# A new order of turns on four engines for a kernel of eight transformer stages

## What is computed

```python
for l in range(4):
    sa, ca, ga, sb, cb, gb = modulation(silu(c[l]) @ wmod[l])     # per batch element
    x = x + ga * attn[l](layernorm(x) * (1 + ca) + sa)
    x = x + gb * ffn[l](layernorm(x) * (1 + cb) + sb)
# attn: 0 decayed linear attention (a scan over tokens, gamma)
#       1 four blocks of causal linear attention with 16 heads of 8, each with a 512-wide MLP
#       2 delta rule with a fixed decay, 3 gated delta rule (both solve a triangular system per chunk)
# ffn:  0 and 1 mixture of 8 experts, 2 of them per token, 2 and 3 one expert per batch element
```

## Time and profile before

| | |
|---|---|
| Median of three runs | 1737.48 us (1735.43 to 1738.29) |
| Span of the profiled execution | 1734.0 us |
| Instructions in the profile | 31,744 |
| PE busy | 1698.0 us, 98% |
| DVE busy | 1234.6 us, 71% |
| POOL busy | 1218.5 us, 70% |
| ACT busy | 1088.9 us, 63% |
| HBM traffic | 22.52 MB read, 2.15 MB written |

### The profile page before, as it was taken

The page is one execution under the profiler, slowest core; times in us unless marked ns, Lnnn a source line. Parts: engine busy times, 40 slices in busy tenths (PEclk is TensorE's granted clock), DMA queues, the critical chain, the costliest instruction groups (busy, mean ns, idle before and its releaser), DMA issues.

```text
span 1734.0 us, 31744 instructions
## 1 busy us (share of the span) xinstructions
PE 1698.0 (98%) x10006; PEld 1300.6 (75%) x10006; DVE 1234.6 (71%) x4490; ACT 1088.9 (63%) x2904; POOL 1218.5 (70%) x1771
## 2 busy tenths in 40 slices
PE   8999999999999999999999999999999899999998
PEld 5788888876667676676666677767788787788976
DVE  7864335688987988988899866445566766578773
ACT  6555226556677678777776786446546666665656
POOL 5655649898878987888789785135347876666667
PEclk9999999999999999999999999999999999999999
DMA  7100000010000000000000000000000001000002
GB/s 254 71 29 1 1 2 3 3 51 1 1 1 1 1 1 1 1 1 1 1 1 1 1 11 6 1 1 7 2 3 3 1 18 31 21 1 2 2 2 73
DMA packets 24027, 26.70 MB, mean 15 GB/s; under 512 B 3492, under 2 KB 20772, under 8 KB 23476
## 3 DMA queue, kind: packets, MB, share of 16 engines
q1 hardware_dynamic: 23860, 24.67, 4.4%
HBM read 22.52 MB, written 2.15 MB: 14 GB/s over the span
## 4 chain that ended last, share of the span: by engine, by line
PE 80%; POOL 6%; DVE 6%; ACT 4%; issue 2%; DMA 0%; SPq 0%; POOLq 0%; ACTq 0%; DVEq 0%
PE ps L87 74%; PE ps L90 7%; POOL arena L104 6%; ACT arena L98 4%; DVE arena L104 2%; DVE arena L110 1%; DVE arena L130 1%; DVE arena L147 1%; ACT arena L99 0%; DVE arena L133 0%; ACT L98 0%; DVE arena L107 0%; DMA arena<-in_x 0%; DVE arena L136 0%; DVE ps L147 0%
## 5 line engine op out<-in xcount | busy, mean ns | idle before, releaser
L104 POOL TENSOR_TENSOR arena<-arena 128x512 f32<-128x512 f32 (+6 forms) x836 | 715.5, 869 | 278.4 <-DVE arena L110 96.9
L98 ACT ACTIVATE arena<-ps 128x128 f32<-128x128 f32 (+11 forms) x1204 | 338.6, 326 | 394.1 <-PE ps L87 287.8
L87 PE MATMUL ps<-arena 128*128 128x128 f32 (+4 forms) x2792 | 441.0, 291 | 10.0 <-DVE arena L104 3.5
L87 PEld LDWEIGHTS ps<-arena 128*128 128x128 f32 x2792 | 373.3, 191 | 97.9 <-issue 46.5
L104 DVE TENSOR_TENSOR arena<-ps,arena 128x128 f32<-128x128 f32 (+4 forms) x696 | 312.9, 468 | 176.0 <-PE ps L87 163.6
L98 ACT ACTIVATE arena<-arena 128x128 f32<-128x128 f32 (+1 forms) x836 | 321.2, 439 | 51.3 <-POOL arena L104 39.6
L87 PE MATMUL ps<-arena,moe 128*128 128x256 f32 (+1 forms) x960 | 288.2, 439 | 0.0
L87 PE MATMUL ps<-arena,cst 128*128 128x504 f32 (+2 forms) x768 | 283.6, 489 | 2.2 <-ACT arena L98 1.1
L98 ACT ACTIVATE arena<-ps,cols 128x512 f32<-128x512 f32 x324 | 216.8, 688 | 103.3 <-PE ps L87 96.5
L104 POOL TENSOR_TENSOR arena<-arena,cst 128x144 f32<-128x144 f32 (+7 forms) x536 | 186.2, 356 | 93.0 <-ACT arena L98 57.4
L110 DVE SCALAR_TENSOR_TENSOR arena<-ps,arena 128x128 f32<-128x128 f32 (+1 forms) x476 | 156.6, 364 | 120.4 <-PE ps L87 94.2
(11 more groups left out here) (120 smaller groups left out, 1756.5 us busy)
## 6 DMA issues: line engine op xcount, KB each, us to landing
rows<-in_rows SPq DMA_DIRECT2D x1, 2253.0 KB, 14.2
arena<-in_x SPq DMA_DIRECT2D x8, 256.0 KB, 5.3
wf<-in_wf SPq DMA_DIRECT2D x2, 1024.0 KB, 6.6
arena<-in_L_ffn_W SPq DMA_DIRECT2D x8, 256.0 KB, 2.9
out_dram<-arena SPq DMA_DIRECT2D x8, 256.0 KB, 2.7
wmod<-in_wmod SPq DMA_DIRECT2D x4, 384.0 KB, 7.7
arena<-kept SPq DMA_DIRECT2D x24, 64.0 KB, 2.9
arena<-kept SPq DMA_DIRECT2D x8, 192.0 KB, 3.0
```

What stands on the lines that cost most here:

```text
L87: return UNSENT if self.e is None else self.e.matmul(out, lhsT, rhs, start=start, stop=stop)
L98: return self.e.activation(out, in_, func, bias=bias, scale=scale)
L104: return UNSENT if self.e is None else self.e.tensor_tensor(out, a, c, op)
```

## The change

The four strings of `TURNS` are replaced, and nothing else. They were found by annealing on durations from a trace, with the SBUF port that VectorE and GpSimd share counted as exclusive, so that two instructions that need it don't run at once. The strings for `pe`, `dve`, `act` and `pool` go from 3333, 3861, 2145 and 1180 digits to 3303, 3831, 2115 and 1150. What falls away are digits whose generator had already ended: every element's work is still emitted in full.

```diff
-    "pe": ("2000000000000120002230001222000112200011100211012003013211003031110332001332322330320113213131222121"
+    "pe": ("0000210000000020003220001222000121010101022010112003011310020111330330201323213203331231130212232111"
```

More of the change, by code:

```diff
@@ new lines @@
+    "act": ("4002440103400202122021211101120333033341123210000033040010100000120032212003302010110020222203202103"
+          "3020112103231213011213223101301122112011113201221021113321211113120223112332301003032103000113000120"
+          "3003120013001030212301300232230010301000202110221032203030011103122333310100200222001212101011200200"
+          "2220203313011231123221202030030302111312333112302302002333031111320311212022231313131110213322022103"
+          "1233323003000013013331113032021222003212200301333311320103301033301033122221212002203020322133011131"
+          "2133023313020223313102121111032301222113230031211000020222311213133231031230021002022003121311130233"
+          "2312223112111000100302323323131012211011102030331302230300222230211131130323113020220011210223033313"
+          "2213030110000013123222230323300310111032210221020130002011100011110203022332101101100210022220211123"
+          "3110302130300020033213222013231111332302223020302302102211311123320210002101322111121303210323330301"
+          "2022122232131111320330200312222022110113231313130232122210302330330310101301113331330322221323102333"
+          "3023011132102032100003023303321222112310002000133120200002201202323031102302000320221231301322022112"
+          "1231113332233032122112111001000121221123221111200300201233332223212203113331112131101032202221002001"
+          "2203003300313010301201023101130023110231011302131021013001103012231033301232202000102322103233010310"
+          "3212300220113010132002332310033333322311231123111221303012223221133121011313103022223320322203210023"
+          "0322022310320202311301311003232331001122330003200332312313202013333300303123200303303333120331220001"
+          "1202113022110112212222011331023022310110323101300032123200313003322131112011300002303330002232233230"
+          "1210103113330201011233121322013320210102231211111203022021131323321223130003121313300123220033112033"
+          "1112333223210131203333100302213331100232231103033221020210320122003313230113120111302330313030333120"
+          "0121020220032001313223310121103313103213132113122011330221332233221313022031220300330222032131022303"
+          "3300210032132101210121003110012313202222110220021123011033030123221303302023113202113221133111233112"
+          "2031233322203110322322333233310331202031233320000012011110113320100132221001122121033223133321323332"
+          "230300222312333"),
```

190 lines of the change are left out of this document (84 added, 106 removed).

## The result

The changed kernel takes **1778.28 us** in the median of four runs (1775.58 to 1778.51), the kernel before 1736.45 in the runs beside it. The ratio is 1.0236, with an interval of 1.0222 to 1.0251, so the change costs 42 us. The forecast was 1729.8, and its range ended at 1744. Both the sign and the size were wrong.

A forecast was written before the change was run, and what follows sets the result against it. PE was taken as the bound, busy for 1698.0 of 1734.0 us. The terms summed to -7.7 us, giving a span of 1726.3 us and, with 3.5 us for the median, 1729.8 us; the range was 1716 to 1744.

The forecast's parts named there:

- New waits: On PE, the reshuffle creates five new waits of 0.45 us among some 2670 waiting places: +2.0 us.
- A: Rival: no change, 1737.0 us; waits move rather than vanish, delays reaching PE through DVE and POOL; chance 0.23.
- Waits with more cover: 31 of PE's 62 waits get more work of other elements ahead of them; half of 18.8 us won: -9.4 us.
- The two named places: PE's waits at the `wo` matmul near 1110 us and the l2 matmul near 1366 us, 0.46 us each, would go.
- Waits with less cover: 9 of PE's 62 waits get less work of other elements ahead of them: +4.0 us.
- Short stalls: Fewer waiting instructions right behind one of their own element, 733 to 629 on PE: -3.0 us.
- The start: ACT's table load moves into its idle time before 14.62 us; PE gains up to 1.0, pays up to 0.4: -0.4 us.
- The shared port: DVE and POOL instructions lengthening each other on SBUF, an estimated 16 us in both engines, would count little: -1.0 us.
- Table loads: Two more table loads of 1.28 us on ACT, which holds 4% of the chain: +0.1 us.
- B: Rival: slower, 1746 us; keeping all port pairs apart delays nearly full POOL from 1340 to 1410 us; chance 0.17.
- C: Rival: much faster, 1715 us; the order takes two thirds of 32.8 us of PE's waits, 22 us; chance 0.10.

The follow-up runs named there:

- r: The old strings with some 175 swaps of neighbouring steps drawn at random and unpriced, 3% of the steps: 1777.79 us.
- h3: The old order for the first 150 us, the changed kernel's order behind it: 1777.4 us.
- g: Strings annealed from the old order with the shared port counted as exclusive for certain DVE and POOL instructions, delays counted in full: 1748.45 us.
- p1: Strings annealed from the old order with PE's round trip alone counted too short: 1799.19 us.
- c: Strings annealed from the old order with the port counted but the round trips of all engines priced short: 1831.11 us.
- a: Strings annealed from the old order on a replay fitted to the traces, with all delays and the shared port counted: 1741.45 us.
- b: Strings annealed from the old order with all delays counted but the shared port left out: 1746.17 us.
- d: Strings annealed from the changed kernel's order instead of the old one, with all delays and the port counted: 1738.26 us.
- e: Strings annealed from the old order with 0.04 us more counted on each handing over between engines: 1742.58 us.
- p2: Strings annealed from the old order with results of DVE, ACT and POOL counted ready too early, PE's round trip in full: 1761.09 us.
- h1: The new order for what the old one starts in its first 867 us, the old order behind it: 1752.93 us.
- h2: The old order for the first 867 us, the new order behind it: 1762.81 us.

## Why the prediction was wrong

**New waits** (+2.0 us, bounds 0 and 18.8) is the step that failed. I took five, and there are 92 newly idle instructions with 44.0 us. With the lateness too short to show as idle, what wasn't a wait before grew by 57.9 us. Even the upper bound was wrong, since it took the waits removed as the measure of those that can be made. The measure should have been the places where one can arise, the "2670 waiting places" of the same paragraph, where r shows how much there is to lose: an unpriced swap of neighbours costs 41.6 / 175 = 0.24 us on average. The new waits arose mostly at producers that found their engine busy with other elements' work (199 of the 271 newly late instructions, 45.6 of 58.4 us). The prediction looked at what stands on PE, and put nothing down for the reshuffled strings of DVE, ACT and POOL, although its rival A names that path.

**Waits with more cover** (-9.4) held, and was even small. By the count of PE instructions since the element's last, 41 of the 93 idle ones have more ahead of them, and their lateness went from 21.4 to 6.3 us, -15.1. The two named places are among them. The `wo` matmul starts without a wait:

```profile
1132.78 0.72 PE L87 MATMUL ps<-moe,arena 128*128 128x128 f32 x5
1133.34 0.39 PE L87 MATMUL ps<-wo,arena 128*128 128x128 f32 x2
```

The l2 matmul of the earlier trace rows does too, inside a run of eighteen:

```profile
1393.04 2.21 PE L87 MATMUL ps<-arena 128*128 128x128 f32 x18
```

But the matmul of element 0 just ahead of it, which had 0.10 us of idle time before it at 1366.36, now waits 0.35 us.

**Waits with less cover** (+4.0) had the wrong sign: 16 instructions, from 5.9 to 5.4 us. What has already waited isn't what a reshuffle makes wait.

**Short stalls** (-3.0) rested on the fall of adjacent waiting places from 733 to 629, and that measure misleads. PE's late instructions rose from 189 to 310 while it fell. It takes an element's cover on PE as whole instructions, of 0.11 us or so each, and ignores what runs on the engine that must supply the next one. Of the 92 newly idle instructions, 49 have less cover than before, but 25 have the same and 18 have more. The example at 1286 us is one of the 18. Among the other engines POOL idles 131.6 us ahead of the layer norms' L104, 128.4 of it for DVE's L147 (93.0 and 89.2 before), and ACT's L98 from SBUF 70.9 instead of 51.3. These rows alone prove little: POOL's idle time grew by 43.8 us in all, about as much as the span, and ahead of its largest group it fell from 278.4 to 252.0.

```profile
L98 ACT ACTIVATE arena<-arena 128x128 f32<-128x128 f32 (+2 forms) x836 | 320.2, 439 | 70.9 <-POOL arena L104 63.5
...
L104 POOL TENSOR_TENSOR arena<-arena,mhalf 128x4 f32<-128x4 f32 (+1 forms) x140 | 150.2, 1073 | 131.6 <-DVE arena L147 128.4
```

**The start** (-0.4) was read right on ACT and wrong on PE. The table load ran where I put it and the second read ended at 15.57 us, before 17.0:

```profile
12.91 1.28 ACT L98 ACT_TABLE_LOAD   x1
14.21 0.20 ACT L98 ACTIVATE gd<-rows 128x1 f32<-128x1 f32 x1
14.32 1.25 ACT L98 ACTIVATE arena<-ps,cols 128x512 f32<-128x512 f32 x2
```

Before, the same stretch of PE was this:

```profile
12.45 3.75 PE L87 MATMUL ps<-arena,w 128*128 128x512 f32 x4 [0.87 <-ACT arena L98]
16.03 0.61 PE L90 MATMUL ps<-cst,arena 128*128 128x128 f32 x4
17.45 0.49 PE L87 MATMUL ps<-w,arena 128*128 128x128 f32 x2 [0.81 <-ACT arena L98]
```

The wait at 17.45 for ACT's second read is gone, and that matmul starts at 15.62. The transposes, at 16.03 before and 15.04 now, gained 1.0 us too, but not by the load. Before, they followed without a wait on the four matmuls of 12.45, which took 3.75 us at a granted clock of 0.50 (from 10 to 14 us; 0.74 from 14 to 18). Those take 1.98 us now, at 1.00, and then PE waits 1.26 us for the first read, which stands behind the load. That the gain came out as large as forecast is luck. Then PE waits longer, 2.00 us at 18.43, and after that its clock is down, which the prediction had excluded from 20 us on. Here are PE's timeline and the windows at the start of the changed kernel:

```profile
11.80 1.98 PE L87 MATMUL ps<-arena,w 128*128 128x512 f32 x4 [0.87 <-ACT arena L98]
...
15.04 0.66 PE L90 MATMUL ps<-cst,arena 128*128 128x128 f32 x4 [1.26 <-ACT arena L98]
15.62 0.49 PE L87 MATMUL ps<-w,arena 128*128 128x128 f32 x2
...
18.43 1.12 PE L90 MATMUL ps<-cst,arena 128*128 128x128 f32 x4 [2.00 <-ACT arena L98]
...
21.27 3.29 PE L87 MATMUL ps<-arena,w 128*128 128x512 f32 x4
```

```profile
10.00:14.00 4.00, 2.92 (x10) 1.10 (x8) 2.22 (x10) 3.49 (x6) 1.08 (x7) 1.00 0.84 207
14.00:18.00 4.00, 1.40 (x9) 1.05 (x9) 3.90 (x31) 2.82 (x8) 2.10 (x6) 0.91 0.18 40
...
20.00:22.00 2.00, 2.00 (x8) 1.61 (x8) 1.55 (x10) 2.00 (x6) 1.11 (x3) 0.50 0.90 229
```

The four matmuls of 128x512 at 21.27 take 3.29 us at a granted clock of 0.50, the lower level (1.2 GHz), where the same four took 1.88 before, at 1.00. The old order had its stretch at 0.50 earlier, from 10 to 14 us. PE is busy for only 1.40 of the 4 us ahead of the fall, and for 3.19 in the old order. The start thus costs 1.9 us by 25 us instead of winning 0.4, and in h3 repairing the head wins 0.9 us in the median.

**The shared port** (-1.0) was about nothing in the sum: the lengthening on DVE is 16.0 us before and 17.9 after. At single places it counts, as at 1282.70 us, where it delays the DVE result that PE waits for. My inference beside it, that a new order only chooses who waits, doesn't hold in g, where the sum of the lengths is 7.1 us shorter since other work stands between such pairs. The rule of the Trainium skill from which I drew it (SBUF — State Buffer, section Who interferes with whom: the second of a pair blocks in full until the first ends) agrees with the longest rows here, 1.3 us where 0.22 is the median. **Table loads** (+0.1) can't be told apart here.

Of the rivals, B had the sign, but not the mechanism: PE's idle time from 1340 to 1410 hasn't grown, POOL is busy there for 57.7 us, and g, which has an exclusive pricing of narrow pairs, doesn't lose 42 us. In g itself, though, that stretch is where over half of the loss arises. A pricing that keeps all pairs apart wasn't timed. C supposed that the order takes nearly all the old waits. A had the mechanism, waits that move over the other engines, and supposed that they would only balance what is won.

What is shown, then: the loss is many small new waits of PE in all parts of the program, most of them for producers whose engine was busy. Orders annealed with PE's round trip underpriced are slow too (p1, c), but they carry 31 us of newly late round trips, where the changed kernel has 7.7 and a 7.1. Orders annealed with every delay counted lose 1 to 12 us (a, b, d, e, g), and p2, which counts PE's round trip and not the others' delays, loses 24. Why the new order was preferred to the old one stays open. That its pricing left out PE's round trip isn't borne out. By my replay's pricing of p1 the new order stands at 1736 us against 1718 for the old one, and by that of c at 1707 against 1697, so neither would have preferred it. Durations that don't hold in the new order, as those of the four L107 above, are a cause that no run tests, and so is p2's error. Also open is where the replay's hope comes from. It was within 8 us of the span for the six orders that no annealing of mine had made (the old one, the change, h1, h2, h3 and r), 13 to 16 too low for c, p1 and p2, 10 for b, and 21 to 29 too low for a, d, e and g (its figures for h1, h2, h3 and g aren't shown). In a, by the replay, 10 of the 25 us are there by 250 us and 10 more come after 1340, and a margin doesn't take them away (e). Exchanging one engine's string alone wasn't tried, since the new string of any one engine beside the old ones of the rest leaves engines waiting for each other without end. So it isn't true, as the front matter has it, that any shuffle computes the same: the four strings must fit each other.

## What to carry to other kernels

A new order can't be judged by following the waits that the old one shows: here it improved those while it made new ones at places that never waited. Nor can it be judged by what stands on the bounding engine alone, since most new waits came from the order on the engines that supply it. Price every place where the bounding engine depends on another, or assume the base rate: here a third of a microsecond for each instruction of PE that comes late, and 0.24 us for a blind swap of neighbours. An annealer may find the errors of its own pricing: mine was within 8 us on orders that it hadn't made and 10 to 29 too hopeful on those that it had, so none counts until it is timed.

## What the runs showed of the hardware

A late matmul costs more than its wait. For 128x128 its second float32 pass mostly follows 0.18 to 0.21 us after the first instead of 0.11, and the profile counts that as busy: 23.0 us of such lateness before, 33.4 after the change, 42.8 in c. PE's round trip has three parts in these traces: the record of a 128x128 result ends 0.163 to 0.165 us after the next instruction of PE may start (the profile models this end, and the semaphore is recorded 0.014 us behind it), DVE or ACT starts 0.033 to 0.042 us after that, and PE starts 0.054 us after their end, or 0.145 at the `wo` matmuls and some others. The other engines overlap their own next instruction by more than such a handing over takes: DVE starts the next 0.084 us before the last one's end is recorded, ACT some 0.10 and POOL 0.042. An estimate that gives each instruction its recorded length therefore counts these engines too slow, and one that takes results as ready when the next may start counts every dependence too fast. p2, which makes the second error for DVE, ACT and POOL, ends 20 us above a.
